# A mixture of 16 experts: four of its eight batches dispatched in 128-row tiles, four left dense

## The chip, the cores and the metric

The kernel runs as one program on one NeuronCore of a Trainium2 chip. The metric is device time in microseconds (us) of one execution. An engine here is one of PE (TensorE, matrix products; PEld is its loading of weights), DVE (VectorE), ACT (ScalarE), POOL (GpSimd) and SP (SyncE, which here only issues DMAs). Each runs its own instructions in order and meets the others at semaphores.

## The reference, cut to what matters

Four residual steps follow one another on `x` of shape (8, 512, 128): a recurrent attention, a mixture of 8 experts with capacity 512, a gated linear attention with an MLP behind it, and a mixture of 16 experts. The change is in the last MLP and the last mixture:

```python
# end of the third step: h2 is a layer norm of x with weights; W1 is 128x256, W2 256x128
x = x + gelu(h2 @ W1 + b1) @ W2 + b2
# fourth step, on layernorm(x); E, K, I = 16, 4, 256
logits = hs @ router_w + router_b
probs = softmax(logits)
topw, topi = top_k(probs, K)
topw = topw / sum(topw)
c = sum over the K choices of one_hot(topi) * topw        # zero for 12 of 16 experts
for each expert e:
    out += (gelu(x @ w1[e] + b1[e]) @ w2[e] + b2[e]) * c[:, e]
```

Every token uses 4 of the 16 experts; for the other 12 its coefficient is zero.

## The kernel before

A batch is 512 tokens, held as four tiles of 128. The residual `resid` stays in SBUF. Matrix products that must be near fp32 are done in f16 parts: a matrix times SCALE (1024) is split into a high and a low f16 half, and three products (high x high, high x low, low x high; `PARTS`) are added up in PSUM.

The last mixture is dense: `all_experts(b)` on each engine goes through the 16 experts for batch `b`, whatever the router chose. One expert for one batch is a unit, 128 units in all. In a unit

- PE `hidden1(b, e)` makes two 128-channel halves of the hidden layer, three products of 512 columns each, with the expert's weights as stationary operand;
- ACT applies gelu to both halves (line 1191), and copies the 128x1024 result to f16, the high half (line 1195);
- POOL subtracts that from the fp32 result, which gives the low half (line 745);
- PE `outputs1(b, e)` makes 24 products of 128 columns into one PSUM bank (four token tiles, three parts, two halves);
- DVE `accumulate(b, e)` (line 1857) adds the four tiles times the token's coefficient to `resid`.

PE is up to three units ahead with `hidden1`; banks 0 to 3 hold hidden halves, 4 and 5 outputs, 6 everything else, 7 small numbers. Four low and high halves are held. All waits are on counting semaphores: `S(name), at(n)` is "the n-th of this kind is done".

Between the units of batch b, at fixed places in the order of each engine, runs the chain that prepares batch b+1: normalise (DVE `normalise11`), transpose (PE), copy (ACT), first MLP product, gelu, split into two f16 halves by DVE (`hT11_low`, `hid11_split`, lines 1747 to 1753), second MLP product, `add_mlp` with statistics and an inverse root by iteration (DVE), `normalise12`, transpose, `x_copies` and `split_x`, the router's product (`logits12`), softmax and the top four (`route_logits`, `route_largest`), and the coefficients (`route_weights`). The bias of all experts is one product of transposed coefficients with the 16 biases, added at unit 14. The first batch does its MLP in fp32 instead. On PE and ACT the batches are a hardware loop (`Fori`), in which the batch enters as a register, so that for instance `x_hl[:, bass.ds(c * (2 * T) + ...)]` is addressed by register; DVE and POOL are written out.

The earlier mixture (8 experts) already dispatches: POOL scatters token rows to a DRAM tensor `disp` by indirect DMAs (`scatter`, line 655), SP reads them back by expert, and outputs are scattered to `y_rows` (line 672) and read back by token by SP (line 527). A helper `mm` issues nearly all matmuls, so that they share line 1909; transposes have line 1916.

## Time and profile before

| | us |
|---|---|
| median of two runs | 952.9 (952.86 and 952.95) |
| span of the profiled execution | 921.2 |
| the runs' median less the span (what lies around it) | 31.7 |
| first gelu of the last mixture, from the span's start | 531.5 |
| PE busy, share of the span | 775.8, 84% |
| DVE busy | 693.3, 75% |
| ACT busy | 628.6, 68% |
| POOL busy | 628.8, 68% |

The profile gives the span of the one execution that it shows, and no time of its own around it. Times in rows are counted from the span's start. A matmul's duration holds the passage through the array, under which the next one already runs. A granted clock of 1.00 is 2.4 GHz.

### The profile page before, as it was taken

To read this page: it belongs to the slowest core of one execution; us is meant where nothing else is said; L and a number is where in the kernel's file an instruction comes from. 1 tells how busy PE (TensorE), PEld (TensorE's weight loads), DVE (VectorE), ACT (ScalarE), POOL (GpSimd) and SP (SyncE) were. 2 spreads that over 40 slices of the span, in tenths; PEclk is the share of its full clock that TensorE was granted. 3 is DMA by queue.
4 is the path that set the end of the run, shared out by engine and by line. 5 is a ranking of instruction groups with operands and counts; after the bars stand their busy time and mean duration, and the time that the engine had idled before them with its cause. 6 is when DMAs were issued, how large, how long until landed. Compare 5 with 4: busy or idle time off the path is not lost.

```text
span 921.2 us, 18395 instructions
## 1 busy us (share of the span) xinstructions
PE 775.8 (84%) x6152; PEld 470.1 (51%) x6152; DVE 693.3 (75%) x2078; ACT 628.6 (68%) x938; POOL 628.8 (68%) x414
## 2 busy tenths in 40 slices
PE   4965765568998789378778989999999999999997
PEld 1343221124453357223233756777677777677775
DVE  7769799994777578598899878766666666666664
ACT  3855233323455567259788988898888888889895
POOL 4008899730477727466888997686868686868695
PEclk9987889999999799769999999999999999999999
DMA  5999300007200030252600000000000000000000
GB/s 149 119 121 207 113 0 0 15 6 194 87 21 7 4 103 25 82 147 50 202 1 1 1 2 2 12 1 11 0 11 0 12 0 0 11 0 11 0 13 13
DMA packets 52792, 40.47 MB, mean 44 GB/s; under 512 B 6059, under 2 KB 44734, under 8 KB 52734
## 3 DMA queue, kind: packets, MB, share of 16 engines
q1 hardware_dynamic: 49662, 37.28, 18.5%
q0 software_dynamic: 3072, 2.51, 1.0%
q8 instruction: 24, 0.39, 0.2%
q14 instruction: 34, 0.28, 0.1%
HBM read 18.07 MB, written 14.88 MB: 36 GB/s over the span
## 4 chain that ended last, share of the span: by engine, by line
POOL 24%; PE 19%; issue 14%; DVE 14%; ACT 6%; DMA 1%; POOLq 0%; DVEq 0%; ACTq 0%; SPq 0%
POOL scratch L745 21%; PE PS L1909 17%; DVE scratch L1670 2%; DVE resid L1572 2%; DVE stats L1407 1%; DVE scratch L1678 1%; POOL resid L731 1%; PE PS L1916 1%; POOL disp L655 1%; ACT scratch L1195 1%; ACT scratch L1191 1%; DVE resid L1420 1%; DVE A L1432 1%; DVE scratch L1410 1%; ACT A L1126 1%
## 5 line engine op out<-in xcount | busy, mean ns | idle before, releaser
L745 POOL TENSOR_TENSOR scratch<-scratch 128x1024 f16<-128x1024 f32 x128 | 272.9, 2134 | 84.5 <-ACT scratch L1195 82.4
L1857 DVE SCALAR_TENSOR_TENSOR resid<-PS,coef,resid 128x128 f32<-128x128 f32 x512 | 144.0, 344 | 108.9 <-PE PS L1909 103.6
L1909 PEld LDWEIGHTS PS<-A,scratch 128*128 128x128 f16 x3456 | 203.4, 98 | 37.8 <-POOL scratch L745 4.8
L1909 PE MATMUL PS<-A,scratch 128*128 128x128 f16 x3456 | 217.1, 219 | 3.9 <-POOL scratch L745 1.6
L1909 PE MATMUL PS<-A 128*128 (+1 forms) x768 | 186.8, 379 | 0.8 <-DVE A L1701 0.2
L1191 ACT ACTIVATE scratch<-PS,cols 128x512 f32<-128x512 f32 x256 | 163.8, 683 | 25.8 <-PE PS L1909 18.9
L1195 ACT ACTIVATE scratch<-scratch 128x1024 f16<-128x1024 f32 x128 | 135.3, 1057 | 5.0
L1909 PE MATMUL PS<-scratch,ident 128*128 128x512 f32 x160 | 88.3, 673 | 52.9 <-DVE scratch L1373 52.9
L614 POOL TENSOR_TENSOR scratch<-A 128x1024 f32<-128x1024 f32 x32 | 76.0, 2383 | 73.8 <-DVE A L1342 56.5
L1909 PEld LDWEIGHTS PS<-A 128*128 128x128 f16 x768 | 70.7, 98 | 66.6 <-issue 0.6
L655 POOL DMA_INDIRECT disp<-A,scratch x64 | 62.9, 982 | 36.5 <-issue 30.2
L1909 PEld LDWEIGHTS PS<-scratch,ident 128*128 128x128 f32 x160 | 30.7, 209 | 100.2 <-DVE scratch L1373 78.1
L1364 DVE TENSOR_TENSOR_SCAN PS<-PS,scratch 128x512 f32<-128x512 f32 x64 | 74.9, 1215 | 1.9
L1909 PE MATMUL PS<-scratch,A 128*128 128x512 f16 (+1 forms) x216 | 52.8, 390 | 1.4 <-DVE scratch L1520 0.7
L672 POOL DMA_INDIRECT y_rows<-A x32 | 34.2, 1070 | 27.6 <-DVE A L1535 23.6
L1916 PE MATMUL PS<-ident,scratch 128*128 128x128 f32 x128 | 21.4, 294 | 33.4 <-ACT scratch L981 15.5
L694 POOL TENSOR_TENSOR scratch<-scratch,A 128x1024 f32<-128x1024 f32 x16 | 38.3, 2394 | 13.1 <-DVE scratch L1670 4.9
L1909 PE MATMUL PS<-scratch,w_r 128*8 128x512 f32 (+1 forms) x106 | 40.2, 509 | 5.9 <-DVE scratch L1753 3.0
L838 ACT ACTIVATE PS<-A 128x512 f32<-128x512 f32 x33 | 19.7, 599 | 35.8 <-DVE PS L1364 35.8
L683 POOL TENSOR_SCALAR A<-resid,scratch 128x128 f32<-128x128 f32 x32 | 31.3, 989 | 18.5 <-DVE scratch L1584 18.5
L838 ACT ACTIVATE PS<-scratch 128x512 f32<-128x512 f32 x31 | 18.6, 601 | 36.6 <-DVE PS L1364 35.5
L1670 DVE TENSOR_TENSOR_SCAN scratch<-PS,scratch 128x512 f32<-128x512 f32 x32 | 37.3, 1206 | 3.1 <-POOL scratch L694 1.2
(336 smaller groups left out, 1330.9 us busy)
## 6 DMA issues: line engine op xcount, KB each, us to landing
A<-A SPq DMA_DIRECT2D x22, 256.0 KB, 7.4
...
```

The costliest lines, as they stand in the source:

```text
L614: pool.tensor_tensor(c_ring[n % 3], bkR[:, 2 * p:2 * p + 2, :], vR[:, i, :].unsqueeze(1).to_broadcast([128, 2, T]), MUL).then_inc(S("r0_c" ...
L655: pool.indirect_dma_start(out=disp[:, :], in_=rows5[RING_OF[b]][:, k, t, :], in_offset=None, out_offset=bass.IndirectOffsetOnAxis(ap=slot_ ...
L672: pool.indirect_dma_start(out=y_rows[:, :], in_=eo[:, ex * NT + t, :], in_offset=None, out_offset=bass.IndirectOffsetOnAxis(ap=xd[:, ex * ...
L694: pool.tensor_tensor(cbuf[n % 2], cs[n % 2], v1[:, bts(b, T)].unsqueeze(1).to_broadcast([128, 2, T]), MUL).then_inc(S("r_c"), 1)
L745: pool.tensor_tensor(h_low[n % 4], h_full[n % 2], h_high[n % 4], SUB).then_inc(S("m1_low"), 1)
L838: A_(bank(n % 2), kk_pair(a, m)[:, max(i, j) % 2, :], ACT.Identity, scale=-1.0, bias=1.0).then_inc(S("r0_decay"), 1)
L1191: A_(h_full[e % 2][:, h * T:(h + 1) * T], bank((e * HC1 + h) % 4), ACT.Gelu, scale=1.0 / SCALE, bias=cols[:, MB1 + e * HC1 + h:MB1 + e * H ...
L1195: A_(h_high[e % 4], h_full[e % 2], ACT.Copy).then_inc(S("m1_high"), 1)
L1364: V.tensor_tensor_scan(out=bank(2 + 2 * (n % 2) + u), data0=bank(u), data1=c_ring[n % 3][:, u, :], initial=0.0, op0=MUL, op1=ADD).then_inc ...
L1670: last = V.tensor_tensor_scan(out=state[:, j, :], data0=bank(2 + j), data1=cbuf[n % 2][:, j, :], initial=0.0, op0=MUL, op1=ADD)
L1857: last = STT(out=resid[:, g, :], in0=bank(4 + e % 2)[:, t * C:(t + 1) * C], scalar=coef[b % 2][:, t, e:e + 1], in1=resid[:, g, :], op0=MUL ...
L1909: return nc.tensor.matmul(o, l, r, start=start, stop=stop)
```

## The change

The last mixture's batches 0, 1, 4 and 7 stay dense. For batches 2, 3, 5 and 6 each token is sent, as a row of 132 words (its normalised channels as f16 high and low parts, and its number), to four slots of a DRAM tensor `disp12`, one for each chosen expert. Each expert has a region of 2048 + 128 rows there. When all four batches are placed, DVE makes a list of 128-row tiles, expert by expert, and 80 tiles (20 groups of four) are worked through. 80 is the most that could be needed; unneeded tiles are run on rows that nobody owns. A group reads its four expert numbers into PE's registers, and takes `w1`, `w2` and the biases at the addresses worked out from them. SP reads the rows' places in the same way. Group outputs are not scaled or added: DVE `evict` copies them to SBUF, POOL scatters them to `y12` by choice and token, SP reads them back at the end, and DVE `combine12` adds four weighted rows per token.

A unit is now a dense (batch, expert) pair or a group. There are 84: 48 dense (batches 0, 1, 4), then groups with one dense unit of batch 7 after every second one until eight of its 16 are left, then those eight. Low halves are made by POOL, but by DVE in the units in which POOL scatters tokens (`SCATTER_AT`, four units each from 18, 23, 33 and 38) and from the first group on. The chain of batch c starts at unit `CHAIN_AT[c]`, every five units, in bank 6 or 7 by turns, and its MLP is fp32 for every batch. All engines' code is written out, without a loop. Small numbers of the router move from PSUM bank 7 to SBUF.

```diff
+        DENSE, SPARSE = (0, 1, 4, 7), (2, 3, 5, 6)
+        ND, NS = len(DENSE), len(SPARSE)
+        CHAIN_AT = (None, -2, 3, 8, 13, 18, 23, 28)
+        ROWS12 = NS * T
+        REGION = ROWS12 + 128
+        NOBODY = E1 * REGION
+        GT = 4
+        LAST_DENSE, COMBINE_BEHIND = 8, 5
+        GROUPS12 = -(-((NS * T * TOP1 + E1 * 127) // 128) // GT)
+        UNITS = [("dense", i, e) for i in range(ND - 1) for e in range(E1)]
+        left = [("dense", ND - 1, e) for e in range(E1)]
+        for g in range(GROUPS12):
+            UNITS.append(("group", g, 0))
+            if g % 2 and len(left) > LAST_DENSE:
+                UNITS.append(left.pop(0))
+        UNITS += left
+        NU = len(UNITS)
+        UNIT_OF_GROUP = [UNITS.index(("group", g, 0)) for g in range(GROUPS12)]
+        LAST_UNIT = [UNITS.index(("dense", i, E1 - 1)) for i in range(ND)]
+        AHEAD, TR_AHEAD, SCATTER_BEHIND = 3, 5, 3
+        XT_RING, YO_RING, XG_RING = 7, 4, 3
+        SCATTER_AT = [CHAIN_AT[b] + 15 for b in SPARSE]
+        LOW_BY_POOL = [not any(f <= u < f + NT for f in SCATTER_AT) and u < UNIT_OF_GROUP[0] for u in range(NU)]
+        LIST_AT = CHAIN_AT[SPARSE[-1]] + 16
+
...
+        def low_made(u):
+
+            n = sum(p == LOW_BY_POOL[u] for p in LOW_BY_POOL[:u])
+            return (S("m1_low"), at(n)) if LOW_BY_POOL[u] else after("m1_low_dve", n)
...
+            for g in range(GROUPS12):
+                if g >= XT_RING:
+                    n = g - XT_RING
+                    sp.wait_ge(*since(s_yo[n % YO_RING], 16 * GT * (n // YO_RING + 1)))
+                first_row = registers(mybir.EngineType.SP, tile_list[:, 128 + GT * g:128 + GT * g + GT], NOBODY)
+                for t, r in enumerate(first_row):
+                    sp.dma_start(xt[g % XT_RING][:, t, :], disp12[bass.ds(r, 128), :]).then_inc(s_xt[g % XT_RING][0], 16)
+            for k in range(YO_RING):
+                sp.wait_ge(*since(s_yo[k], 16 * GT * len(range(k, GROUPS12, YO_RING))))
+            sp.wait_ge(S("x_b2"), at(B - 1))
+            sp.wait_ge(S("xn"), 2 * B + at(B - 1))
+            yv12 = y12.rearrange("(k s n p) c -> s p k n c", k=TOP1, s=NS, p=128)
+            for i in range(NS):
+                for k in range(TOP1):
+                    sp.dma_start(y2[i][:, k, :, :], yv12[i][:, k, :, :]).then_inc(s_y2[i][0], 16)
...
+            def scatter_tokens(i, n):
+                if n == 0:
+                    pool.wait_ge(*after("slots12", i))
+                    pool.wait_ge(*after("lo12", i))
+                    pool.wait_ge(*since(s_copies[i], 16 * (TOP1 - 1)))
+                    pool.wait_ge(*after("ids12", i))
+                for k in range(TOP1):
+                    pool.indirect_dma_start(out=disp12[:, :], in_=rows12[i][:, k, n, :], in_offset=None,
+                                            out_offset=bass.IndirectOffsetOnAxis(ap=slot12[i][:, n, k:k + 1], axis=0),
+                                            bounds_check=NOBODY - 1, oob_is_err=False).then_inc(s_rows12[0], 16)
+
+            def scatter_outputs(g):
+                pool.wait_ge(S("m1_acc"), at(UNIT_OF_GROUP[g]))
+                pool.wait_ge(*since(s_xt[g % XT_RING], 16 * GT * (g // XT_RING + 1)))
+                for t in range(GT):
+                    pool.indirect_dma_start(out=y12[:, :], in_=yo[g % YO_RING][:, t, :], in_offset=None,
+                                            out_offset=bass.IndirectOffsetOnAxis(
+                                                ap=xt[g % XT_RING][:, t, ID:ID + 1].bitcast(i32), axis=0),
+                                            bounds_check=TOP1 * ROWS12 - 1, oob_is_err=False).then_inc(s_yo[g % YO_RING][0], 16)
+
+            for u in range(NU):
+                if LOW_BY_POOL[u]:
+                    low_half(u)
+                if u in (1, 2):
+                    low_weights(B - 3 + u)
+                for c in range(2, B):
+                    if u == CHAIN_AT[c]:
+                        add_up(c)
+                for i in range(NS):
+                    if u == max(SCATTER_AT[i] - 10, 3):
+                        token_ids(i)
+                    if SCATTER_AT[i] <= u < SCATTER_AT[i] + NT:
+                        scatter_tokens(i, u - SCATTER_AT[i])
+                if u >= SCATTER_BEHIND and UNITS[u - SCATTER_BEHIND][0] == "group":
+                    scatter_outputs(UNITS[u - SCATTER_BEHIND][1])
...
+            def group_channels(g):
+                act.wait_ge(*after("xg_tr", g))
+                if g >= XG_RING:
+                    act.wait_ge(S("m1_hid_mm"), at(2 * UNIT_OF_GROUP[g - XG_RING] + 1))
+                A_(xg[g % XG_RING], bank(6 + g % 2).bitcast(f16), ACT.Copy).then_inc(S("xg_copied"), 1)
...
+            def hidden_parts(u):
+                kind, i, e = UNITS[u]
+                if u >= 2:
+                    act.wait_ge(*low_made(u - 2))
+                for h in range(HC1):
+                    act.wait_ge(S("m1_hid_mm"), at(2 * u + h))
+                    if kind == "dense":
+                        A_(h_full[u % 2][:, h * T:(h + 1) * T], bank((2 * u + h) % 4), ACT.Gelu, scale=1.0 / SCALE,
                            bias=cols[:, MB1 + e * HC1 + h:MB1 + e * HC1 + h + 1]).then_inc(S("m1_hid"), 1)
...
+                act.wait_ge(S("m1_out_mm"), at(u, 4))
+                A_(h_high[u % 4], h_full[u % 2], ACT.Copy).then_inc(S("m1_high"), 1)
...
+            def route_rows(i):
+
+                TT(weight12[i], top1[:, :, 0:TOP1], over(share, TOP1), MUL)
+                st.done(spread_picks())
+                dve.wait_ge(*after("counts12", i, 1))
+                V.tensor_copy(picked12.rearrange("p (n e) -> p n e", e=E1), picked_P).then_inc(S("picked12"), 1)
+
+            def low_rows(i):
+                dve.wait_ge(*after("hi12", i))
+                TT(rows12_16[i][:, 0, :, C:2 * C], xn12, rows12_16[i][:, 0, :, 0:C], SUB).then_inc(S("lo12"), 1)
+
+            def place_rows(i):
+
+                dve.wait_ge(*after("counts12", i))
+                counts = chain_bank(SPARSE[i])
+                st.done(TT(place12, counts[:, 0:NT * E1].rearrange("p (n e) -> p n e", e=E1),
+                           carry12.unsqueeze(1).to_broadcast([128, NT, E1]), ADD))
+                TT(carry12, carry12, counts[:, NT * E1:NT * E1 + E1], ADD).then_inc(S("placed12"), 1)
+                st.done(TT(one_hots, one_hots, place12.unsqueeze(2).to_broadcast([128, NT, TOP1, E1]), MUL))
+                st.done(V.tensor_reduce(out=idx_P, in_=one_hots, axis=AX, op=ADD))
+                V.tensor_copy(slot12[i], idx_P).then_inc(S("slots12"), 1)
+
...
+            def evict(u, g):
+                dve.wait_ge(S("m1_out_mm"), at(u))
+                if g >= YO_RING:
+                    dve.wait_ge(*since(s_yo[g % YO_RING], 16 * GT * (g // YO_RING)))
+                TS(yo[g % YO_RING], bank(4 + u % 2).rearrange("p (n c) -> p n c", c=C), 1.0 / SCALE, None,
+                   MUL).then_inc(S("m1_acc"), 1)
+
+            def low_half(u):
+                dve.wait_ge(S("m1_high"), at(u))
+                dve.wait_ge(S("m1_out_mm"), at(u, 4))
+                TT(h_low[u % 4], h_full[u % 2], h_high[u % 4], SUB).then_inc(S("m1_low_dve"), 1)
+
...
+            def combine12(i):
+                dve.wait_ge(*since(s_y2[i], 16 * TOP1))
+                for k in range(TOP1):
+                    for t in range(NT):
+                        g = SPARSE[i] * NT + t
+                        last = STT(out=resid[:, g, :], in0=y2[i][:, k, t, :], scalar=weight12[i][:, t, k:k + 1],
+                                   in1=resid[:, g, :], op0=MUL, op1=ADD)
+                    if k < TOP1 - 1:
+                        st.done(last)
+                last.then_inc(S("y_combined"), 1)
+
...
+                n = u - NU + LAST_DENSE - COMBINE_BEHIND
+                if 0 <= n < NS:
+                    combine12(n)
+                if u == LIST_AT - 1:
+                    list_tiles()
+                if u == LIST_AT:
+                    list_out()
+            for i in range(max(0, LAST_DENSE - COMBINE_BEHIND), NS):
+                combine12(i)
...
             def hidden11(c, h):
-                if isinstance(c, int):
-                    if h == 0:
-                        pe.wait_ge(S("xT_copied"), 3 * B + at(c))
-                    if h == 1:
-                        pe.wait_ge(S("hid11"), at(2 * c))
-                    mm(bank(6), tile(u_1, h), hT11).then_inc(S("hid11_mm"), 1)
-                    return
-                if h == 0:
-                    pe.wait_ge(S("xT_low"), 2 * B + at(c, 1))
-                if h == 1:
-                    pe.wait_ge(S("hid11_low"), at(2 * c, 2))
-                for k, (sw, sx) in enumerate(PARTS):
-                    last = mm(bank(6), tile(u1_hl[:, sw, :], h), hT11_hl[:, sx, :], start=k == 0, stop=k == len(PARTS) - 1)
-                last.then_inc(S("hid11_mm"), 1)
+                pe.wait_ge(S("xT_copied"), 3 * B + at(c))
+                chain_bank_read(c)
+                mm(chain_bank(c), tile(u_1, h), hT11).then_inc(S("hid11_mm"), 1)
+                read_by[c % 2] = S("hid11"), at(2 * c + h)
 
...
+                weights_at[i] = registers(mybir.EngineType.PE, tile_list[:, GT * i:GT * i + GT], (E1 - 1) * HC1 * 128)
+                pe.wait_ge(*after("xg_copied", i))
+                if i == 0:
+                    pe.wait_ge(*since(s_b12, 16 * 6))
+                x = xg[i % XG_RING]
                 for h in range(HC1):
-                    n = (b * E1 + e) * HC1 + h
-                    pe.wait_ge(S("m1_hid"), at(n, 4))
-                    w = slice((e * HC1 + h) * 128, (e * HC1 + h) * 128 + 128)
-                    for k, (sw, sx) in enumerate(PARTS):
-                        last = mm(bank((e * HC1 + h) % 4), w1_hl[:, sw, w], x_hl[:, bass.ds(b * (2 * T) + sx * T, T)],
-                                  start=k == 0, stop=k == len(PARTS) - 1)
+                    pe.wait_ge(S("m1_hid"), at(2 * u + h, 4))
+                    for t, w in enumerate(weights_at[i]):
+                        out = tile(bank((2 * u + h) % 4), t)
+                        for k, (sw, sx) in enumerate(PARTS):
+                            mm(out, w1_hl[:, sw, bass.ds(w + h * 128, 128)], tile(x, sx * GT + t), start=k == 0, stop=False)
+                        last = mm(out, b12[:, bass.ds(w + h * 128, 128)], ones_b[:, 0:128], start=False, stop=True)
                     last.then_inc(S("m1_hid_mm"), 1)
 
-            def outputs1(b, e):
-                n = b * E1 + e
-                pe.wait_ge(S("m1_low"), at(n))
-                pe.wait_ge(S("m1_acc"), at(n, 2))
-                for t in range(NT):
+            def outputs1(u):
+                kind, i, e = UNITS[u]
+                pe.wait_ge(*low_made(u))
+                pe.wait_ge(S("m1_acc"), at(u, 2))
+                for t in range(NT):
+                    out = tile(bank(4 + u % 2), t)
                     for k, (sh, sw) in enumerate(PARTS):
                         for h in range(HC1):
-                            w = slice((e * HC1 + h) * 128, (e * HC1 + h) * 128 + 128)
-                            part = (h_high, h_low)[sh][e % 4][:, h * T + t * 128:h * T + t * 128 + 128]
-                            last = mm(tile(bank(4 + e % 2), t), part, w2_hl[:, sw, w],
-                                      start=k == 0 and h == 0, stop=k == len(PARTS) - 1 and h == HC1 - 1)
+                            w = slice((e * HC1 + h) * 128, (e * HC1 + h) * 128 + 128) if kind == "dense" else bass.ds(weights_at[i][t] + h * 128, 128)
+                            part = (h_high, h_low)[sh][u % 4][:, h * T + t * 128:h * T + t * 128 + 128]
+                            last = mm(out, part, w2_hl[:, sw, w], start=k == 0 and h == 0,
+                                      stop=kind == "dense" and k == len(PARTS) - 1 and h == HC1 - 1)
+                    if kind == "group":
+                        last = mm(out, ones_b[:, 128:256], b12[:, bass.ds(weights_at[i][t], 128)], start=False, stop=True)
                 last.then_inc(S("m1_out_mm"), 1)
 
...
+            def group_transposed(g):
+                pe.wait_ge(*since(s_xt[g % XT_RING], 16 * GT * (g // XT_RING + 1)))
+                chain_bank_read(g)
+                x16 = A7[:, GT * RW * (g % XT_RING):GT * RW * (g % XT_RING + 1)].bitcast(f16).rearrange("p (n c) -> p n c", c=2 * RW)
+                for s in range(2):
+                    for t in range(GT):
+                        last = nc.tensor.transpose(tile(bank(6 + g % 2).bitcast(f16), s * GT + t), x16[:, t, s * C:s * C + C], ident16)
+                last.then_inc(S("xg_tr"), 1)
+                read_by[g % 2] = after("xg_copied", g)
+
```

## Rows read from the trace of the kernel before

**Rows 1.** The page: the span in 40 slices, busy tenths of PE.
```profile
PE   4965765568998789378778989999999999999997
```
**Rows 2.** Windows: us, busy time and instructions by engine, granted clock, DMA share, GB/s.
```profile
585.22:633.05 47.83, 47.47 (x544) 34.59 (x542) 32.90 (x129) 42.46 (x57) 36.56 (x18) 1.00 0.02 6
...
531.50:585.20 53.70, 48.61 (x521) 34.68 (x520) 41.70 (x187) 44.10 (x60) 42.88 (x24) 1.00 0.01 2
531.50:921.20 389.70, 376.34 (x4264) 274.07 (x4262) 263.74 (x1058) 336.13 (x445) 296.39 (x148) 1.00 0.02 6
```
**Rows 3.** Windows, one unit with no chain step on PE; columns as before.
```profile
636.67:639.30 2.63, 2.63 (x33) 1.92 (x31) 2.53 (x11) 2.52 (x4) 2.44 (x2) 1.00 0.00 0
```
**Rows 4.** Timeline of one unit: start, us, engine, line, what.
```profile
700.07 1.46 PE L1909 MATMUL PS<-A 128*128 x6
700.08 1.25 ACT L1191 ACTIVATE scratch<-PS,cols 128x512 f32<-128x512 f32 x2
...
701.36 1.50 PE L1909 MATMUL PS<-A,scratch 128*128 128x128 f16 x24
701.36 1.06 ACT L1195 ACTIVATE scratch<-scratch 128x1024 f16<-128x1024 f32 x1
```
**Rows 5.** Waits in the batch 633.05 to 680.89: us in total, times, longest.
```profile
DVE resid L1857 <- PE PS L1909: 12.6, 10, 2.5
...
PEld PS L1909 <- DVE scratch L1753: 0.5, 1, 0.5
```
**Rows 6.** Timeline of PE, the first batch's MLP in fp32.
```profile
515.88 1.12 PE L1909 MATMUL PS<-scratch,u 128*128 128x512 f32 x2
516.84 1.05 PE L1909 MATMUL PS<-u_o,A 128*128 128x128 f32 x8
...
519.68 2.05 PE L1909 MATMUL PS<-u,scratch 128*128 128x128 f32 x16
```
**Rows 7.** Groups of DVE, batch 633.05 to 680.89: busy, mean ns, idle before.
```profile
L1857 DVE SCALAR_TENSOR_TENSOR resid<-PS,coef,resid 128x128 f32<-128x128 f32 x64 | 18.0, 343 | 13.3 <-PE PS L1909 12.6 <-DVE scratch L1714 0.6
L1753 DVE TENSOR_TENSOR scratch<-PS,scratch 128x512 f16<-128x512 f32 x2 | 1.4, 691 | 0.1
L1752 DVE CAST scratch<-PS 128x512 f16<-128x512 f32 x2 | 1.4, 686 | 0.3 <-ACT PS L1138 0.3
...
L1747 DVE SCALAR_TENSOR_TENSOR scratch<-PS,cols,scratch 128x512 f16<-128x512 f32 x1 | 0.7, 743 | 0.0
```
**Rows 8.** Line 655 and its timeline: landing, and two DMAs in a row.
```profile
DMA to landing us min/median/max: 2.1/2.1/3.3
...
245.68 0.97 POOL L655 DMA_INDIRECT disp<-A,scratch  x1 [0.31 <-issue]
246.95 0.97 POOL L655 DMA_INDIRECT disp<-A,scratch  x1 [0.30 <-issue]
```
**Rows 9.** Timeline of DVE and POOL in the earlier mixture.
```profile
339.72 1.21 DVE L1501 SCALAR_TENSOR_TENSOR A<-A 128x1024 f16<-128x1024 f32 x1
340.04 1.74 POOL L672 DMA_INDIRECT y_rows<-A  x1 [0.30 <-DVE A L1535]
```
**Rows 10.** Groups of POOL, batch 633.05 to 680.89.
```profile
L745 POOL TENSOR_TENSOR scratch<-scratch 128x1024 f16<-128x1024 f32 x16 | 34.1, 2134 | 11.2 <-ACT scratch L1195 11.0
L731 POOL TENSOR_TENSOR resid<-resid,A 128x512 f32<-128x512 f32 x1 | 1.3, 1281 | 0.0
```
**Rows 11.** Line 1909 from 578.90 to 579.95: ns min, median, max, first and last start.
```profile
L1909 PE MATMUL PS<-coef,A x12: 169/169/181, 579.6 to 579.9; 128*128 128x16 f16 x12
L1909 PEldq FUSED_REGOPS  x8: 46/46/65, 578.9 to 579.8; - x8
```
**Rows 12.** Line 527, reads by token: ns, first and last start, landing.
```profile
L527 SPq DMA_DIRECT2D A<-y_rows x14: 359/507/510, 387.0 to 400.3; - x14
...
DMA to landing us min/median/max: 3.1/3.5/4.8
```
**Rows 13.** Timeline, DVE's last accumulation.
```profile
915.41 1.12 DVE L1857 SCALAR_TENSOR_TENSOR resid<-PS,coef,resid 128x128 f32<-128x128 f32 x4
```

592 lines of the change are left out of this document (391 added, 201 removed).

## The prediction

> **What bounds the kernel now.** I read the page's busy shares and its forty slices first: the last 17 slices are one steady pattern, PE at 9 tenths [rows 1]. That is the last mixture, 128 units of one expert and one batch each. It starts at the first gelu (531.5) and lasts 389.7 us to the end of the span. Then I cut it by batch. A middle batch takes 47.83 us and PE is busy for 47.47 of it at a granted clock of 1.00, while DVE is busy for 32.90, ACT for 42.46 and POOL for 36.56 [rows 2]. One unit with nothing else between takes 2.63 us, all of it PE [rows 3]. That is six 512-column matmuls and 24 of 128 columns, which start 0.216 and 0.056 us apart (1.46 us for the six and 1.50 for the 24, each with a tail of 0.16 under which the next already runs [rows 4]). So 16 units are 42.1 us, and the chain that prepares the next batch (normalise, small MLP, router) adds 5.7 us of PE to each batch. The waits agree: DVE waited 12.6 us for PE in a batch and POOL 11.0 for ACT, while PE's longest was 0.5 [rows 5, 10]. The page's chain that ended last names POOL L745 first. I don't follow it: POOL idles 11 us per batch. PE is the bound, with ACT (2.31 us per unit: two gelus and a copy [rows 4]) not far behind.
>
> The stage adds up as 53.7 for the first batch, 6 x 47.83, and 49.0 for the last one and the end of the span [rows 2]. The profile's span is 921.2 us and the runs' median 952.9, so 31.7 us lie outside the span and I carry them over.
>
> **The change part by part.** Work goes from 128 units to 84: 64 dense ones, and 20 groups of four 128-row tiles.
>
> Dense units: 64 x 2.63 = 168.3 us on PE.
>
> The chain's MLP in fp32. The first batch already runs it so. Each of its two 512-column products holds PE for 0.96 us (515.88 to 516.84, where the next begins), and the sixteen 128-column records for 2.05 less the last one's tail of 0.16 [rows 6]. That is 3.8 us against 6 x 0.216 + 24 x 0.056 = 2.6 for the f16 form, so +1.2. PE's waits for DVE's splits (0.5 [rows 5]) and the loop's own cost go, sparse batches lose two small products and gain eight count products. I take 6.0 us per chain, 42 for seven. Those who lose work are DVE's three splits, 3.5 us per batch [rows 7]. Nothing waited for them longer than that.
>
> Chains now start every 5 units, so in the first 48 units PE has 48 x 2.63 + 42 = 168 us, 3.5 per unit. DVE has 4 x 0.281 = 1.13 per accumulation, and per chain 32.9 - 18.0 - 3.5 = 11.4 us [rows 2, 7], about 12.5 with the counting of rows. POOL is the one I watch. A sparse batch adds 16 indirect DMAs, which came 1.28 us apart with nothing waited for [rows 8]: 20.5 us, during which DVE makes the four low halves (1.2 us each, by the 128x1024 row [rows 9]). The scatters start at units 18, 23, 33 and 38, so there are two stretches of nine units in which POOL has 32 x 1.28 + 2 additions (2.55 each) + one low half of 2.13 = 48.2 us [rows 8, 10]. PE has 9 x 2.63 + 9/48 x 42 = 31.6 there. POOL's next low half is wanted by ACT two units on and by PE after that, so I let it be 5 us late free of charge: 11.6 us of stall per stretch, 23 for both. The first 48 units come to 191. Bounds: no stall at all (168), and the whole excess (201). The first batch took 5.9 more than a middle one [rows 2]; its extra work (weight splits, statistics) stays, +6.
>
> The list of tiles, the clearing of tails and the first loads: POOL's last scatter ends some 25 us after it starts, near unit 42, a DMA lands after 2.1 us [rows 8], the load after 3 more, and PE wants the first group at unit 43. I take 2 us of stall, between 0 and 12.
>
> A group on PE: 32 hidden and 28 output products of 128 columns, 60 x 0.056 = 3.35 us, and 8 transposes, 0.45. But their weights are addressed by register. The one place where the trace has register-addressed weights is the router's twelve products: eight register operations (46 ns busy each) run from 578.9 to 579.8, 0.13 us apart, with 12 products to 8 operations, so two products behind one of them cost no more than one [rows 11]. With products of only 16 columns the array caught up with it. A group needs six different addresses per tile in the hidden part (high and low weights and the bias, twice) and five in the output part: 44. At 0.12 (the two ends are rounded, so a little under 0.13 is as likely) that is 5.3 us, more than the array's 3.35. So groups are paced by PE's sequencer, not its array. Bounds: 3.8 us (array alone) and 60 x 0.13 + 0.45 = 8.25.
>
> Loading four registers per group from SBUF has no row. Below: four register operations of 0.05 (0.2 us) [rows 11]. Above: the quickest DMA's landing, 2.1 [rows 8]. It stays on the core like the register operations, without a DMA, so it is nearer to them; I take 0.4. The group is 5.3 + 0.45 + 0.4 = 6.15 us, 123 for twenty. The Trainium skill (DMA: Bandwidth & Descriptors, Latency and other measured facts) gives a floor of about 600 ns for such a load, and its page Runtime: NRT & Kernel Launch (Instruction fetch mechanics) some 200 ns per register; by these the sum would be 4 to 8 us more. No run so far shows it.
>
> Beside it: ACT has 2.31 + 1.06 for the copy of transposed rows, DVE 0.69 [rows 7] + 1.2, POOL 4 x 1.28 = 5.1 for the scatter of outputs, which is below 6.15. Eight dense units between the groups are 21 us.
>
> The end. After the last group, eight dense units, 21 us. From there POOL's scatter takes 5.1, landing 2.1, and then 16 reads of 256 KB, issued 1.02 us apart where the kernel does this now (14 from 387.0 to 400.3), 3.5 to land [rows 12]: the last lands 27 us after the last group. Three of the four combinations, each of 16 x 0.281 = 4.5 us sit between DVE's last accumulations, and the fourth after them: 15.8 (six units) + 4 x 4.5 + 2 x 1.2 = 36.2, against 22.7 for the dense units with their last accumulation: +13.5. What follows, 4.7 us from the last accumulation (916.5) to the end of the span, stays [rows 13].
>
> Sum: 191 + 6 + 2 + 123 + 21 + 21 + 13.5 + 4.7 = 382.2 against 389.7: -7.5. Earlier stages lose and gain single small instructions; the POOL constant removed at the start of the kernel and the new masks are both beside other work; if that cover were gone they would be 2 to 3 us. Forecast: 952.9 - 7.5 = 945.
>
> **The rivals.** 2% is 19 us, about what a measurement of this kernel can tell from no change.
>
> Register addressing is hidden. For it: PE's sequencer ran 0.6 us ahead of the array at the router's products, and in dense units it is ahead all the time. Against it: a lead of 0.6 us doesn't pay for 44 operations. Then groups take 3.8 us and POOL's 5.1 paces the last four: 20 x 2.35 - 5 = 42 us less, 903.
>
> POOL is never late. If the low halves wanted after each scatter have more slack than I give, the 23 us of stalls go: 922, also faster.
>
> Slower: registers. The place is the start of each group in PE's queue. If the load costs the round trip of 2.1 us, a group is 7.85 us; if each product (not each address) costs 0.13, it is 8.65. That is 34 or 50 us more: 979 to 995. It decides from 7.5 us per group. For it: the trace has twelve such products in a row, never 60, and no load. Against it: the 0.13 did not grow with two products.
>
> DVE's bunches. Up to four chains are open at once, and their 12.5 us per five units fall mostly on three of the five, some 5 us each with the accumulation, while PE may run only two units ahead. At 4 us per chain: +28, 973. Against it: outside the scatter stretches DVE has 5 x 1.13 + 12.5 = 18.2 us of work where PE has 19.2.
>
> POOL and DVE in each other's way. An indirect DMA of 0.97 us took 1.74 where it started under DVE's 1.21 us operation on SBUF alone [rows 9]. With 16 low halves moved to DVE just there, 16 x 0.77 = 12 us: 957. The Trainium skill (SBUF — State Buffer, SBUF: two separate sides) has it as a rule that a VectorE operation with two SBUF inputs and a GpSimd one that reads SBUF lock each other out. By that rule the trace agrees for one form of operation; the low halves’ own form beside a scatter is in no row.
>
> That the groups do less work is no rival: all 20 are run, full or not.
>
> **How the numbers follow.** The forecast with the mild rivals around it (945, 957): 0.38. Registers hidden (903): 0.26. POOL never late (922): 0.12. Registers dear (979 to 995): 0.14. DVE's bunches (973): 0.10. Faster by over 2% (below 934): 0.26 + 0.12 and a little of the forecast's spread, 0.40. Slower (above 972): 0.14 + 0.10, 0.24, and 0.36 between. The range takes in 903 and the nearer half of the dear side, and leaves out what lies past both: 900 to 985. As the cases have both signs, the forecast's own range is 932 to 962.
>
> **What would show it.** PE's time per group near 6 us, with weight loads starting 0.09 us apart and not 0.056; register operations 0.12 apart; clock still 1.00 (it was at this PE load). In the two scatter stretches ACT and PE idle, ended by POOL's low half. The first group transposed within 5 us of PE asking. DVE last, in four combinations, with PE long done. It is wrong if groups take under 5 us, if PE idles in the first 18 units, or if the loads of rows end most of PE's waits.

## The result and the profile after

The changed kernel takes 1127.0 us (two runs, 1123.05 and 1130.89) against 952.9: ratio 1.182, 95% interval [1.172, 1.192]. I had said 945. Two more groups of runs gave 1.187 [1.182, 1.192] and 1.186 [1.179, 1.194].

The first view is the page of the changed kernel, in forty slices. The last mixture starts in slice 20. Where [rows 1] had nines, PE now has fives to sevens for twelve slices, the granted clock is mostly 7 or 8 tenths, and POOL is idle for most of the time. So in these slices no engine has become the bound: they wait for each other.

```profile
PE   5847755897868727788777657775667799999981
...
POOL 2048986035663546788765332646064624344450
PEclk9987899999979979989868778877869787688986
```

Cut into the parts of my sum (first 48 units; 20 groups with 8 dense units; last eight units and the end), with the columns of [rows 2]:

```profile
570.90:894.00 323.10, 218.40 (x1764) 147.51 (x1763) 206.34 (x729) 157.54 (x207) 153.79 (x116) 0.80 0.11 33
894.00:1064.50 170.50, 167.40 (x1557) 110.52 (x1554) 57.54 (x93) 81.56 (x103) 66.53 (x65) 0.82 0.19 50
1064.50:1121.30 56.80, 30.06 (x309) 20.17 (x306) 37.71 (x107) 17.32 (x23) 16.20 (x16) 0.79 0.38 105
```

I had 197, 146 and 39. In the first part PE stands still for 323.1 - 218.4 = 104.7 us, and its 218.4 busy us are 50 more than the 168 of work that I counted, at a granted clock of 0.80. The waits of that part (us, times, longest) name who is late:

```profile
PE PS L2228 <- DVE scratch L1950: 24.4, 7, 8.2
...
PE PS L2221 <- DVE scratch L1988: 12.9, 2, 6.6
PE PS L2228 <- DVE scratch L1988: 12.5, 2, 6.2
```

L1950 is `normalised` (its result is transposed next) and L1988 the router's logits, which the next chain's transposes in the same PSUM bank must let DVE read first. DVE is late, though it is busy for only 206 of 323 us. Its timeline, and POOL's beside it, show something that no row of before has:

```profile
646.26 0.16 DVE L1944 TENSOR_TENSOR scratch<-scratch 128x4 f32<-128x4 f32 x1
646.46 1.97 DVE L1945 TENSOR_TENSOR scratch<-scratch 128x4 f32<-128x4 f32 x1
648.46 1.19 DVE L1946 SCALAR_TENSOR_TENSOR scratch<-scratch 128x4 f32<-128x4 f32 x1
...
646.29 2.12 POOL L895 TENSOR_TENSOR scratch<-scratch 128x1024 f16<-128x1024 f32 x1 [2.53 <-ACT scratch L1399]
648.37 1.25 POOL L883 TENSOR_TENSOR resid<-resid,A 128x512 f32<-128x512 f32 x1
```

A product of four columns takes 1.97 us: it starts under POOL's low half and ends with it. The next takes 1.19 and ends with POOL's addition. The diff has one line for this, which I had passed over: `P7`, the router's small numbers, moved from PSUM bank 7 to SBUF, because the overlapping chains need both bank 6 and bank 7.

### The profile page after: what moved, and what is told of

It is laid out like the page before. It is cut to its first block and busy times, and to the rows that moved or that the text cites. A ratio compares the mean times of both kernels' runs of the same rounds, so it can differ in the third digit from the quotient of the medians.

```text
span 1121.3 us, 17521 instructions
## 1 busy us (share of the span) xinstructions
PE 830.7 (74%) x5510; PEld 481.6 (43%) x5510; DVE 740.5 (66%) x1948; ACT 550.4 (49%) x824; POOL 570.3 (51%) x468
## 5 line engine op out<-in xcount | busy, mean ns | idle before, releaser
L2221 PE MATMUL PS<-A,scratch 128*128 128x128 f16 (+1 forms) x2400 | 189.3, 237 | 33.6 <-issue 15.5
L2221 PEld LDWEIGHTS PS<-A,scratch 128*128 128x128 f16 x2400 | 161.5, 107 | 68.3 <-issue 39.7
L2221 PE MATMUL PS<-A 128*128 128x128 f16 (+1 forms) x864 | 180.5, 336 | 4.0 <-issue 3.3
L2113 DVE SCALAR_TENSOR_TENSOR resid<-PS,coef,resid 128x128 f32<-128x128 f32 x256 | 71.9, 344 | 137.4 <-remote 69.7
L1392 ACT ACTIVATE scratch<-PS,cols 128x512 f32<-128x512 f32 x128 | 83.2, 685 | 74.8 <-PE PS L2221 42.1
L895 POOL TENSOR_TENSOR scratch<-scratch 128x1024 f16<-128x1024 f32 x32 | 68.2, 2136 | 85.1 <-ACT scratch L1399 80.8
L909 POOL DMA_INDIRECT disp<-A,scratch x64 | 65.4, 1023 | 83.0 <-DVE scratch L2047 64.8
L2221 PEld LDWEIGHTS PS<-A 128*128 (+1 forms) x864 | 72.2, 107 | 74.3 <-issue 43.4
L800 POOL DMA_INDIRECT disp<-A,scratch x64 | 62.6, 978 | 54.1 <-issue 30.6
L1399 ACT ACTIVATE scratch<-scratch 128x1024 f16<-128x1024 f32 x84 | 88.8, 1057 | 2.7
L2228 PE MATMUL PS<-ident,scratch 128*128 128x128 f32 x128 | 25.7, 336 | 84.8 <-DVE scratch L1950 32.1
L2127 DVE TENSOR_TENSOR scratch<-scratch 128x1024 f16<-128x1024 f32 x52 | 63.4, 1219 | 1.6 <-issue 0.9
L1395 ACT ACTIVATE scratch<-PS 128x512 f32<-128x512 f32 x40 | 23.4, 596 | 52.2 <-PE PS L2221 36.2
```

Of the source, the lines that this page charges most:

```text
L800: pool.indirect_dma_start(out=disp[:, :], in_=rows5[RING_OF[b]][:, k, t, :], in_offset=None, out_offset=bass.IndirectOffsetOnAxis(ap=slot_ ...
L895: pool.tensor_tensor(h_low[u % 4], h_full[u % 2], h_high[u % 4], SUB).then_inc(S("m1_low"), 1)
L909: pool.indirect_dma_start(out=disp12[:, :], in_=rows12[i][:, k, n, :], in_offset=None, out_offset=bass.IndirectOffsetOnAxis(ap=slot12[i][: ...
L1392: A_(h_full[u % 2][:, h * T:(h + 1) * T], bank((2 * u + h) % 4), ACT.Gelu, scale=1.0 / SCALE, bias=cols[:, MB1 + e * HC1 + h:MB1 + e * HC1 ...
L1399: A_(h_high[u % 4], h_full[u % 2], ACT.Copy).then_inc(S("m1_high"), 1)
L2113: last = STT(out=resid[:, g, :], in0=bank(4 + u % 2)[:, t * C:(t + 1) * C], scalar=coef[i % 2][:, t, e:e + 1], in1=resid[:, g, :], op0=MUL ...
```

## The experiments

Six kernels start from the kernel before or repeat it or the changed one; the rest edit the changed kernel. The groups of runs fell on chips on which the kernel before takes different times: 946.5 (first group), 924.0 (second), 952.6 and 952.5 (third and fourth), 951.2 (last). Times are compared within a group, ratios are to the kernel before in the same group.

**Loops written out.** In the kernel before:
```diff
-            with pe.Fori(0, B - 1) as b:
+            for b in range(B - 1):
                 all_experts(b, False)
```
(and ScalarE's loop likewise).

> The kernel before with the last mixture's loops on TensorE and ScalarE written out (batches 0 to 6 as plain code), nothing else changed: the same instructions run in the same order. Theory A (the much longer written-out code of the changed kernel delays instructions, so that even the stages ahead of the last mixture took 37 us more there): this kernel is slower too, by 20 to 40 us ahead of the mixture and a few us in it, 975 to 1000 us. Rival B (the code's length costs nothing; the early 37 us have another cause): within 5 us of 952.9.

942.8 us, ratio 0.997 [0.995, 0.999]. Rival B: the code's length costs nothing. In this execution the first gelu of the last mixture starts at 553.8, where the kernel before has 531.5 with the same instructions ahead of it.

**fp32 MLP alone.** In the kernel before, `hidden11` and `outputs11` take the fp32 form for every batch, and the three splits go.

> The kernel before with the last MLP of every batch in fp32, as the change has it, and without VectorE's three splits for each batch. By my prediction's sum the fp32 products cost what the f16 ones did and DVE gains 3 x 7 instructions of a batch that are off the bound: 950 to 955 us. Rival (the fp32 products take PE longer than the split ones, 2 x 1.7 us + 8 x 0.22 against 3 x 0.21 x 2 + ...): up to 7 batches x 3 us = 21 us slower, 974 us.

946.6, ratio 1.000 [0.999, 1.002]. That term of my sum holds.

**Small numbers in SBUF alone.** In the kernel before:
```diff
-        P7 = bank(7)
+        P7 = carve(8)[:, 0:512]
```

> The kernel before with the router's small numbers in SBUF instead of PSUM bank 7, as the change has them, and nothing else. Theory C (VectorE's small products with both inputs in SBUF are held up by GpSimd's low halves, 1.97 us in place of 0.16 us in the changed kernel's trace, and through the chain of the router they hold up TensorE): slower by 7 batches x some 5 us = 35 us at most where PE waits for the chain, 960 to 990 us, and L1747 rows (the small products) of 1 to 2 us. Rival: the rows are stretched, but nobody waits for them since the chain has 16 units for its steps here: 953 to 956 us.

1063.7, ratio 1.125 [1.123, 1.127]: this one line costs 117 us, far more than the range I had allowed it (960 to 990), though the small products average 0.78 us and not the 1 to 2 that I expected. The mixture takes 494.6 us against 384.8 with the loops written out. PE stands still for 85.5 us of it instead of 12.1, mostly until DVE's accumulations, and is busy for 36 more at a granted clock of 0.91 instead of 1.00 (the largest of its waits for another engine, from 640 to 1040: us, times, longest):

```profile
PE PS L1909 <- DVE resid L1857: 64.2, 13, 6.9
```

From the groups of DVE in the mixture (busy us, mean ns), first with SBUF, then, from the kernel with the loops written out (all else as before, lines one lower), with PSUM:

```profile
L1728 DVE TENSOR_TENSOR scratch<-scratch 128x4 f32<-128x4 f32 x18 | 14.0, 776 | 0.6
...
L1813 DVE CAST coef<-scratch 128x64 f16<-128x64 f32 x7 | 13.0, 1862 | 0.0
```

```profile
L1727 DVE TENSOR_TENSOR PS<-PS,scratch 128x4 f32<-128x4 f32 (+1 forms) x24 | 4.1, 173 | 0.8
...
L1812 DVE CAST coef<-PS 128x64 f16<-128x64 f32 x8 | 1.7, 214 | 0.0
```

Not only instructions with two SBUF inputs are held up. A cast has one input, and two in a row take 2.16 us each while POOL makes two low halves (timeline, kernel with SBUF):

```profile
709.10 2.16 DVE L1812 CAST coef<-scratch 128x64 f16<-128x64 f32 x1
711.18 2.16 DVE L1813 CAST coef<-scratch 128x64 f16<-128x64 f32 x1
...
709.09 4.19 POOL L745 TENSOR_TENSOR scratch<-scratch 128x1024 f16<-128x1024 f32 x2
```

**Fixed weights.** In the changed kernel:
```diff
-                weights_at[i] = registers(PE, tile_list[:, GT * i:GT * i + GT], ...)
+                weights_at[i] = [((GT * i + t) % E1) * HC1 * 128 for t in range(GT)]
```

> The changed kernel with fixed expert numbers in TensorE's products of the 20 groups (no register is loaded or used by PE; the tiles are multiplied with the wrong experts' weights, of the same shape). Theory D (registers cost PE what the prediction put: 5.3 us of arithmetic in all + 20 x 0.4 of loading): faster than the changed kernel's 1127 by some 10 us, 1117. Rival E (register loads and address arithmetic are what made the groups 8.4 us instead of 6.15): faster by 40 us, 1085. Rival F (hidden): 1127.

1106.7, ratio 1.170 [1.166, 1.174], 11 to 16 us below the changed kernel's by the ratios of its three groups. That is nearer to D's 10 than to E's 40, but the granted clock in the groups differed too, so the times alone don't price the registers. The same edit on the next kernel's base is read below.

**Small numbers back in PSUM.** The changed kernel, with `P7` in bank 2 from the mixture on, and the hidden units' ring cut to banks 0, 1 and 3:
```diff
-        P7 = carve(8)[:, 0:512]
+        P7 = bank(2)                        # logits and exponentials stay in SBUF
-                ... bank((2 * u + h) % 4)
+                ... bank((0, 1, 3)[(2 * u + h) % 3])
```

> The changed kernel with the router's small numbers (inverse deviations, sums, picks, coefficients, places) in PSUM bank 2 in the mixture, for which the hidden units' ring is cut from four banks to three; logits and exponentials stay in SBUF. In the kernel before the move to SBUF alone cost 117 us. Theory C (the held-up small instructions are the bulk of the slowdown): 1127 - 100 to 117 = 1010 to 1027 us, with the first 48 units in some 220 us instead of 320. Rival G (the overlapping chains with spacing 5 would hold PE anyway, or three hidden banks cost as much): above 1080 us.

1013.4, ratio 1.097 [1.095, 1.099]. It read like a full success of theory C, but the first 48 units take 270.4 us and not the 220 expected, and part of the rest was the chip, as its second run shows further down. The changed kernel itself was not run on this chip, so what this edit and the next gain there has no number.

**Low halves by VectorE**, small numbers left in SBUF:
```diff
-        LOW_BY_POOL = [not any(...) and u < UNIT_OF_GROUP[0] for u in range(NU)]
+        LOW_BY_POOL = [u < 2 for u in range(NU)]
```

> The changed kernel with the low halves of all units but the first two made by VectorE, none by GpSimd; the small numbers stay in SBUF. Theory C's mechanism (a small VectorE instruction waits because GpSimd works at the same time, not because its operands are in SBUF): the 128x4 products fall from 1.2 to 2 us back to 0.16 us, and the kernel becomes 60 to 110 us faster although DVE takes over 36 low halves more of some 1.3 us (46 us of work): 1020 to 1070 us. Rival H (SBUF operands are slow by themselves): the rows stay at 1.2 us or more and the kernel gets slower by up to 46 us, 1130 to 1170.

1022.8, ratio 1.110 [1.105, 1.115]. H falls: the same instruction on the same SBUF operands is back at 162 ns once POOL makes no low halves (groups of DVE, 543.9 to 820, the line whose instruction took 1.97 above), and the cast from SBUF to SBUF takes 186 ns.

```profile
L1945 DVE TENSOR_TENSOR scratch<-scratch 128x4 f32<-128x4 f32 x21 | 3.4, 162 | 0.7
...
L2023 DVE CAST coef<-scratch 128x64 f16<-128x64 f32 x4 | 0.7, 186 | 0.0
```

**Both edits together.**

> Both edits together: small numbers in PSUM, and low halves by VectorE. Theory C: with the numbers in PSUM the second edit only adds 46 us of work to DVE, so this one is no faster than the one with the numbers in PSUM alone, 1010 to 1060 us. Rival (other instructions of VectorE are held up by GpSimd as well, or hold it up): faster than it by over 2%, below 1000 us.

1020.2, ratio 1.103 [1.101, 1.105]. As theory C has it, the second edit gains nothing once the numbers are in PSUM (it costs 7 us), and the rival, below 1000 us, falls.

**The kernel before once more.**

> The kernel before once more, for a trace: the one I predicted from has a span of 921.2 us where the timed runs had 952.9 us. If what lies around the span is a constant 31.7 us, as I took it, the time stands 31.7 us above the span again. Rival: the profiled execution was a fast one, and the time stands some 2 us above the span (then 21 us of the 37 us by which the changed kernel reached its last mixture late are no effect of the change).

Its own time is 925.05 us with a span of 922.9. What lies around the span is 2 us, not the 31.7 that I carried: the profile I predicted from was of an execution of some 923 us. That is an error of the base, and it also explains 22 of the 38 us by which the changed kernel reached its last mixture late: its first gelu starts at 569.5, against 531.5 in the kernel before and 553.8 for the same instructions elsewhere. Against that execution, of its own group, the kernel with only `P7` moved is 11 us late there (564.7).

**The changed kernel, and two wider spacings of the chains** (on the kernel with the small numbers in PSUM):
```diff
-        CHAIN_AT = (None, -2, 3, 8, 13, 18, 23, 28)
+        CHAIN_AT = (None, -2, 4, 9, 15, 20, 26, 31)     # groups after 52 units
```

> The changed kernel once more, timed beside the others of this group, since the kernel before differs by up to 3% between groups of runs (924 to 953 us). Ratio to the kernel before 1.17 to 1.20, and some 180 us in the 28 units from the first group on if its groups are slow by themselves; Rival: those 28 units come nearer to the 145 us of the kernel with the small numbers in PSUM, since the granted clock of 0.73 to 0.88 there was this execution's.

> The kernel with the small numbers in PSUM, and the router chains started 5 to 6 units apart (-2, 4, 9, 15, 20, 26, 31 instead of -2, 3, 8, 13, 18, 23, 28), so that a chain's logits no longer stand just ahead of the transposes of the chain after next in the same PSUM bank; for that the groups start after 52 units instead of 48, with the same 84 units in all. Theory J (PE's in-order waits for the chains' steps, 67 us of gaps in the first 48 units, come from chains that share a bank too closely): 20 to 40 us faster than the kernel with the small numbers in PSUM, ratio to the kernel before 1.055 to 1.075. Rival K (the waits are of steps of one chain for its own VectorE steps, whatever the spacing): the same within 8 us, 1.09 to 1.10.

> As the kernel with the wider chains, but 6 units apart (-2, 4, 10, 16, 22, 28, 33), groups after 54 units. Theory J: fewer waits still, though 6 apart sets the dense chains' logits (12 units into a chain) beside the transposes of the chain after next: 1.05 to 1.075. Rival K: 1.09 to 1.10.

> The kernel with the small numbers in PSUM, and fixed expert numbers in TensorE's products of the 20 groups (no register is loaded or used by PE). My sum's price of the registers is 13 us (20 x (44 x 0.12 us of arithmetic hidden behind nothing... in my sum 5.3 us in all a group's 44 operations) so that a group is 6.15 us with them and about 4.9 to 5.3 us by its products alone): 15 to 20 us faster than the kernel with the small numbers in PSUM. Rival F (the registers' work lies beside the products): the same within 3 us. Rival E (dearer than put): 30 us or more.

On one chip: the changed kernel 1131.4 (1.187), wider 1097.0 (1.154 [1.148, 1.160]), 6 apart 1114.7 (1.168 [1.160, 1.176]), fixed weights 1087.0 (1.140 [1.136, 1.144]). The kernel with fixed weights has the first 48 units of the kernel with the numbers in PSUM unchanged. So its window and that of the wider one compare the spacing, with the spacing of 5 units first (in the wider one the last chain starts three units later, and some of its steps, 41 of PE's 1764 records, fall behind unit 48). The third line is from the same kernel's groups, the fourth from those of the kernel 6 apart:

```profile
571.10:872.20 301.10, 219.04 (x1764) 147.94 (x1762) 172.77 (x731) 157.43 (x207) 152.90 (x116) 0.80 0.12 36
```

```profile
568.30:835.40 267.10, 194.33 (x1723) 135.06 (x1722) 169.12 (x704) 153.15 (x205) 152.74 (x116) 0.86 0.12 36
...
950.00:1050.00 100.00, 98.94 (x708) 60.80 (x706) 21.87 (x26) 34.87 (x44) 43.66 (x43) 0.57 0.15 43
```

```profile
1000.00:1050.00 50.00, 50.00 (x347) 31.18 (x346) 9.12 (x10) 16.91 (x21) 20.76 (x20) 0.50 0.18 52
```

Theory J holds for that part: 34 us less, 9 of PE's idle time and 25 of its busy time, with the clock at 0.86 instead of 0.80. The third line tells why the total hardly shows it: in the groups PE is busy all the time at a granted clock of 0.57. Six apart is worse still, with 0.50 there. Both ratios lie outside what J and K allowed, since both were set from the other chip's 1.097.

Fixed weights are 15 us below the 1101.6 that the kernel with the numbers in PSUM takes on this chip (below). That is the 15 to 20 of my sum, but not for its reason, as the next views show: its groups with eight dense units take 161.8 us at a granted clock of 0.88, against 175.2 at 0.81 with registers.

```profile
872.20:1034.00 161.80, 157.28 (x1558) 104.62 (x1555) 57.06 (x90) 81.09 (x105) 68.66 (x65) 0.88 0.19 52
```

**What paces a group.** Timelines of PE in a group, first with registers and then with fixed addresses (both at the full clock):

```profile
923.16 0.34 PE L2235 MATMUL PS<-A 128*128 128x128 f16 x3
923.44 0.22 PE L2235 MATMUL PS<-nr,spread_then_b 4*128 4x128 f16 x1
923.60 0.34 PE L2235 MATMUL PS<-A 128*128 128x128 f16 x3
```

```profile
1000.06 0.34 PE L2235 MATMUL PS<-A 128*128 128x128 f16 x3
1000.33 0.22 PE L2235 MATMUL PS<-nr,spread_then_b 4*128 4x128 f16 x1
1000.49 0.34 PE L2235 MATMUL PS<-A 128*128 128x128 f16 x3
```

It is 0.44 and 0.43 us for four products, with and without registers. The three full ones start about 0.06 apart, but the bias product with 4 rows starts 0.15 after the third and the next full one 0.16 after it. So the time goes at the product with 4 rows; whether the few rows cost it or the change between numbers of rows, no run separates. Padded to 128 rows:

```diff
-        b12 = spread_then_b12[0:4, :].bitcast(f16)
+        b12 = spread_then_b12[:, :].bitcast(f16)     # rows 4 to 127 zero
-        ones_b = late[0:4, 128:256].bitcast(f16)
+        ones_b = late[:, 128:256].bitcast(f16)
```

> The changed kernel on the same chip as the three that follow, since the kernel before took 924 us in one group of runs and 953 in two others: 1.18 to 1.19 of the kernel before if the ratio is the same everywhere; lower, about 1.15, if part of the slowdown is a lower granted clock on some chips (Theory L).

> The changed kernel with the router's small numbers in PSUM once more, beside the changed kernel. Theory C (VectorE's small instructions are held up by GpSimd, and this is the largest single part of the loss): 60 us or more faster than the changed kernel on the same chip. Rival M (once the chains are crowded, PE waits for them nearly as long without the hold-ups): 15 to 40 us.

> The kernel with the small numbers in PSUM, and the groups' bias products on 128 rows (four rows of values, the rest zeros) instead of 4 rows. In the trace a 4-row product starts 0.14 us after the product ahead of it and the next one 0.15 us after it, where full products follow each other after 0.056, with fixed addresses just as with registers. Theory N (this, not the registers, paces the groups: a half tile takes 0.43 us, 12 such products a group): a half tile takes 0.22 us, a group on PE 3.8 instead of 6.3 us, GpSimd's scatter (5.1 us a group) paces then, and the kernel is some 40 us faster than the one with the small numbers in PSUM. Rival D (my prediction's: 44 register operations a group at 0.12 pace it): the same within 5 us.

> All three edits: small numbers in PSUM, chains 5 to 6 units apart, bias products on 128 rows. Theory J and N together: 20 to 35 us faster than the one with the bias products on 128 rows, about 75 faster than the one with the small numbers in PSUM, and still no faster than the kernel before. Rival L (groups fall to a lower granted clock as they did with the wider chains, 0.51 to 0.80): no faster than the one with the bias products on 128 rows.

On one chip: the changed kernel 1129.6 (1.186), numbers in PSUM 1101.6 (1.156 [1.151, 1.162]), bias products on 128 rows as well 1086.4 (1.138 [1.131, 1.144]), wider chains as well 1066.3 (1.119 [1.114, 1.124]). Rival M is right: in the changed kernel the hold-ups (less what the smaller ring costs) come to 28 us, not 117. Without them PE still stands still for 80.5 of the first 297.0 us, against 106.8 of 327.7 with them. Theory N is half right, 15 us instead of 40. The group's timeline with 128 rows says why:

```profile
886.62 0.38 PE L2236 MATMUL PS<-A 128*128 128x128 f16 x3
886.88 0.22 PE L2236 MATMUL PS<-nr,spread_then_b 128*128 128x128 f16 x1
887.00 0.35 PE L2236 MATMUL PS<-A 128*128 128x128 f16 x3
```

Four products now take 0.36 to 0.38 us and not 0.22, and the profile has three register operations for each four, 0.12 to 0.13 apart. So just under the limit by rows probably lies the one that I had named; both at once (128 rows and fixed addresses) was not run. A whole group at the full clock takes 6.21 us against 6.34:

```profile
886.62:892.83 6.21, 6.16 (x65) 4.84 (x66) 2.24 (x3) 2.12 (x3) 3.91 (x4) 1.00 0.08 24
...
872.30:1029.60 157.30, 140.76 (x1560) 112.77 (x1558) 56.95 (x90) 80.68 (x103) 68.11 (x65) 0.92 0.20 54
```

That is some 3 us for twenty groups (an estimate from these two windows). The stage became 18 us shorter than the 175.2 with 4 rows. So most of the gain came with the clock, 0.92 instead of 0.81, and why it rose is not shown.

The kernel with the numbers in PSUM ran on two chips, and its windows show what a chip does. First where the kernel before takes 924 us (with one group, 923.16 to 929.50), then where it takes 952.5:

```profile
542.80:813.20 270.40, 202.18 (x1764) 139.82 (x1763) 173.42 (x731) 156.08 (x207) 154.88 (x116) 0.85 0.14 41
813.20:958.00 144.80, 144.76 (x1557) 98.97 (x1554) 56.66 (x90) 81.30 (x104) 73.40 (x65) 0.98 0.21 57
958.00:1010.00 52.00, 26.47 (x308) 19.23 (x305) 37.82 (x107) 17.36 (x22) 16.74 (x16) 0.81 0.43 115
923.16:929.50 6.34, 6.34 (x69) 4.27 (x69) 2.17 (x3) 2.25 (x3) 3.85 (x4) 1.00 0.28 76
```

```profile
573.50:870.50 297.00, 216.53 (x1763) 145.69 (x1762) 172.68 (x731) 157.44 (x206) 153.97 (x116) 0.81 0.12 36
870.50:1045.70 175.20, 170.33 (x1554) 111.38 (x1552) 56.83 (x90) 81.16 (x104) 67.60 (x66) 0.81 0.17 48
```

The same groups take 144.8 us at a clock of 0.98 and 175.2 at 0.81.

**GpSimd's scatter stretches.** In the kernel with all three edits PE stands still for 11.65 us while POOL issues its scatters 1.28 apart and ACT waits for the low half behind them (timeline, POOL, then ACT, then PE):

```profile
680.19 0.99 POOL L923 DMA_INDIRECT disp<-A,scratch  x1 [0.15 <-issue]
681.49 0.97 POOL L923 DMA_INDIRECT disp<-A,scratch  x1 [0.30 <-issue]
...
697.43 1.27 ACT L1406 ACTIVATE scratch<-PS,cols 128x512 f32<-128x512 f32 x2 [14.66 <-POOL scratch L909]
...
698.18 1.46 PE L2238 MATMUL PS<-A 128*128 128x512 f16 x3 [11.65 <-ACT scratch L1406]
```

In all, ACT waits there for POOL's low halves for 39.2 us:

```profile
ACT scratch L1406 <- POOL scratch L909: 39.2, 4, 14.7
```

In the changed kernel that wait is 3.6 us in the whole first part. There PE waits mostly for DVE, and on this chip the wait for POOL grows only with the wider spacing (with the small numbers in PSUM alone it is 3.5 us here and 32.1 on the chip of the second group). The last two kernels have DVE make six low halves there, and the second fills one wait of each chain:

```diff
-        LOW_BY_POOL = [not any(f <= u < f + NT ...
+        LOW_BY_POOL = [not any(f <= u < f + 6 ...
```
```diff
             def transpose12(c):
+                for _ in range(12):
+                    mm(chain_bank(c), ones16[:, :], pickg[:, 0].rearrange("p k n -> p (k n)"))
                 pe.wait_ge(S("xn12"), at(c))
```

> The kernel with all three edits (small numbers in PSUM, chains 5 to 6 apart, bias products on 128 rows), and VectorE makes the low halves of six units from each token scatter on instead of four, since GpSimd's 16 scatters take 20.5 us there. This is the stall term of my prediction (23 us for both stretches); in the trace of that kernel PE stands still for 11.6 and 7.5 us there. Theory P (GpSimd's lateness is what stops PE there): the two gaps shrink to under 3 us each and the kernel is 15 to 30 us faster than the one with the three edits, ratio 1.09 to 1.105. Rival Q (VectorE, now with the low halves and two chains, is late instead): 1.115 to 1.13.

> As the one before it, with 12 products of 512 columns that nobody reads ahead of each chain's second transposes, where PE waits for VectorE anyway (7 chains, 84 products of 0.216 us at the full clock, 18 us of work). Theory L (the lower granted clock, 0.80 to 0.93 in the first 52 units, follows PE's pauses and costs 20 to 35 us there): the clock rises and the kernel gains 5 us or more in spite of the added work. Rival R (the pauses' own length is all they cost, or the filling is too short to change the clock): 5 to 15 us slower.

1049.8, ratio 1.104 [1.100, 1.108], and 1049.4, 1.105 [1.100, 1.110]. Theory P: 1.119 to 1.104 is 15 us (on another chip, with the kernel before within 0.2%), ACT's wait for POOL falls from 39.2 to 5.5 us, and PE's longest pause for ACT there is 2.4 us where it had 11.65 and 7.5. The first 48 units, with the three edits, then with the low halves, then filled:

```profile
570.10:837.40 267.30, 194.44 (x1723) 134.98 (x1722) 169.00 (x704) 153.14 (x205) 152.69 (x116) 0.86 0.12 36
```

```profile
569.70:818.80 249.10, 193.75 (x1735) 134.10 (x1734) 177.24 (x705) 153.96 (x204) 140.09 (x107) 0.88 0.12 37
```

```profile
569.10:824.80 255.70, 205.29 (x1814) 138.78 (x1813) 176.93 (x706) 153.69 (x206) 145.24 (x109) 0.91 0.12 37
```

PE's idle time falls from 72.9 to 55.4 us. The filling raised the clock from 0.88 to 0.91, made this part 6.6 us longer in these two profiles and changed the total by nothing: 18 us of added work were absorbed, without a gain. Neither L's gain of 5 us nor R's loss of 5 to 15 is seen, and how much the clock costs stays open. No version beat the kernel before.

## Why the prediction was wrong, step by step

**What lies around the span** was carried as 31.7 us; it is 2. It moved the forecast's level, not the difference.

**Dense units and the MLP in fp32** were right (2.64 us for a dense unit between groups, from 900.24 to 902.88, and ratio 1.000 for the MLP alone).

**A part of the change had no term.** "Earlier stages lose and gain single small instructions" covered the diff's line on `P7`. Alone it costs 117 us, in the changed kernel 28 in the mixture (1.186 to 1.156), and 11 of the 38 ahead of it. My rival of POOL and DVE in each other's way priced this for 16 low halves beside scatters only (12 us). The Trainium skill (SBUF — State Buffer, Who interferes with whom) says that copies and casts can enter a two-port mode as well and then contend with GpSimd. By that rule the trace agrees: the cast takes 2.16 us beside POOL, 0.21 with its input in PSUM and 0.19 from SBUF to SBUF without POOL's low halves.

**"In the first 48 units PE has 168 us"** is the step that failed most: 323 to 328 measured. The 168 was right as work at the full clock, and I took PE's order as if its steps were always ready, and the clock as 1.00 where 0.80 was granted. On the chip with the fourth group the 328 go down to 297 with the numbers in PSUM and to 267 with the chains 5 to 6 apart. My rival "DVE's bunches" named the place and priced it at 28 us with a chance of 0.10. It looked at DVE's load (18.2 of 19.2 us) and not at the order: a chain's step on PE stands in the queue 1 or 2 units after the DVE step that it needs, and two chains share a bank.

**The scatter stretches**, 23 us: not in the changed kernel, where ScalarE waits for POOL's low halves for 3.6 us in the first part and PE mostly for DVE. With the wider spacing the term is there: the two gaps (11.65 and 7.5) are at the two places I named, and 15 us went with two more low halves by DVE.

**The list**, 2 us within 0 to 12: with the low halves by VectorE, PE's first transposes of a group waited 10.8 us for rows (the waits of that kernel, 780 to 830: PE L2749 for the DMA from `disp`, once, 10.8), in the changed kernel 0.8.

**A group of 6.15 us**: 6.34 at the full clock, and 144.8 us for the stage where I had 144. The number was right by luck, as the cause is only second in line: the 4-row bias products set 0.43 per half tile, the registers probably 0.37. What was missing is the clock, for which I had said 1.00: 170 to 176 us where 0.80 to 0.82 is granted. The register load, taken as 0.4, is 0.33, and hidden (line 504, ns min, median, max):

```profile
L504 PEldq TENSOR_LOAD <-nr x20: 328/333/511, 888.8 to 1054.6; - x20
```

**The end**, 13.5 us: right. The window of the end (56.8 us in the changed kernel, 52.0 at best, where my sum has 39) begins at a ScalarE instruction of the first of the eight units, 15 us before DVE has copied out the last group. From that copy to the end of the span it is 41.8 us, and my path had 36.2 + 4.7 = 40.9 (39.2 of it in the sum). DVE's rows, from the timeline of the changed kernel, are nearly what I described. The combinations start 18.6 us after the last group (I had 15.8), with nothing waited for, and take 20.4 with the two accumulations between, as I had; only two of the four, not three, stand before the last accumulation:

```profile
1078.86 0.69 DVE L2121 TENSOR_SCALAR A<-PS 128x512 f32<-128x512 f32 x1 [1.43 <-PE PS L2221]
...
1098.13 4.66 DVE L2142 SCALAR_TENSOR_TENSOR resid<-A,scratch,resid 128x128 f32<-128x128 f32 x16
1102.70 1.12 DVE L2113 SCALAR_TENSOR_TENSOR resid<-PS,coef,resid 128x128 f32<-128x128 f32 x4
...
1109.34 9.23 DVE L2142 SCALAR_TENSOR_TENSOR resid<-A,scratch,resid 128x128 f32<-128x128 f32 x32
```

**The sum again**, for the run at 1.186 (177 us over before): first 48 units 328 - 197 = +131, groups 176 - 146 = +30, the last window 55.5 - 39 = +16 (by the cut, the last groups' outputs are in it), ahead of the mixture +8 to 11, against my -7.5: about +180. Of it the runs took away 28 (small numbers), 15 (bias), 20 (spacing), 15 (low halves), the clock's changes included. The remaining 99 is shown only by its place: PE still idles 55 us in the first 48 units, the clock is 0.88 there, and the last window stays 13 to 17 longer than my 39. That the range left it out is due to taking the cases as rivals of each other, where several came together, and to the line on `P7` and the clock having no term.
